# Routing and experts in one block, narrow expert blocks alternating with wide ones, and a head's first query job behind its second score group

## The reference

```python
xn = _layernorm(x, axis=-1)
# attention: 8 query heads of width 128 over one shared key/value head, causal, with a position table
q = (xn @ Wq + bq) + pe;  k, v = split(xn @ Wkv + bkv);  k = k + pe
probs = softmax(where(causal, (q @ k.T) / sqrt(128), -inf));  s = concat_heads(probs @ v) @ Wo
# mixture of 8 experts, the best 2 per token
logits = xn @ router_w + router_b;  gating = softmax(only the top 2 logits)
h = relu(xn @ w1[e] + b1[e]);  y = h @ w2[e] + b2[e]      # 256 -> 1024 -> 256
g = silu(sum over the two experts of gating * y)
out = x + s * g
```

## Time and profile before

| | |
|---|---|
| median of 3 runs (lowest, highest) | 1114.44 us (1110.93, 1115.57) |
| the profiled execution, its span | 1122.9 us, 1121.1 us |
| routing | 0 to 88.8 us |
| experts | 88.8 to 483.1 us |
| attention, with its tail from 1084 on | 483.1 to 1121.1 us |
| TensorE busy, share of the span | 1016.8 us, 91% |
| VectorE busy | 883.5 us, 79% |
| ScalarE, GpSimd busy | 554.5 us, 442.7 us |

### The profile page before, as it was taken

The page is one execution under the profiler, slowest core; times in us unless marked ns, Lnnn a source line. Parts: engine busy times, 40 slices in busy tenths (PEclk is TensorE's granted clock), DMA queues, the critical chain, the costliest instruction groups (busy, mean ns, idle before and its releaser), DMA issues.

```text
span 1121.1 us, 28441 instructions
## 1 busy us (share of the span) xinstructions
PE 1016.8 (91%) x10270; PEld 811.9 (72%) x10270; DVE 883.5 (79%) x1607; ACT 554.5 (49%) x1264; POOL 442.7 (39%) x499
## 2 busy tenths in 40 slices
PE   2536999999999999998989889999999999999997
PEld 1525888888888898755666667667777777777776
DVE  6894676676676454479999999998999999999972
ACT  3812223323323333346766666656666666666740
POOL 0013999899995100012323233333333333333331
PEclk9999999999999999998999999999999999999999
DMA  8547666756665512129987898988999888999993
GB/s 280 184 174 152 171 170 172 185 162 178 180 166 145 95 44 49 30 71 161 170 139 145 135 172 159 159 148 156 161 172 179 144 151 149 166 161 159 171 160 105
DMA packets 405896, 169.02 MB, mean 151 GB/s; under 512 B 348634, under 2 KB 396324, under 8 KB 405124
## 3 DMA queue, kind: packets, MB, share of 16 engines
q1 hardware_dynamic: 348704, 127.05, 57.0%
q10 hardware_dynamic: 50580, 22.45, 8.8%
q0 software_dynamic: 6480, 17.70, 7.4%
HBM read 51.66 MB, written 30.67 MB: 73 GB/s over the span
## 4 chain that ended last, share of the span: by engine, by line
DVE 27%; PE 20%; ACT 4%; issue 3%; DMA 2%; SPq 1%; ACTq 0%; DVEq 0%
DVE b_ph L1353 10%; DVE b_nmax L1314 8%; PE b_psO L1137 7%; PE b_psS L1118 5%; DVE b_outs L1361 2%; PE b_psJ L1075 2%; PE b_psJ L1151 2%; DVE b_psJ L1323 2%; ACT b_pr L1217 2%; PE b_psS L1162 2%; DMA b_pT<-b_ph 2%; ACT b_ph L1249 1%; PE b_psS L1075 1%; DVE b_Q L1337 1%; DVE b_f L1367 1%
## 5 line engine op out<-in xcount | busy, mean ns | idle before, releaser
L1442 POOL TENSOR_SCALAR b_ph<-b_pr,b_rrec 128x896 f16<-128x896 f32 (+4 forms) x160 | 109.3, 691 | 502.3 <-DVE b_rrec L1343 460.6
L938 ACT ACTIVATE h<-psU,bias 128x256 f32<-128x256 f32 (+1 forms) x320 | 125.1, 448 | 294.5 <-PE psU L858 170.4
L1217 ACT ACTIVATE b_pr<-b_psS,b_nmax 128x1024 f32<-128x1024 f32 (+7 forms) x256 | 187.3, 736 | 159.0 <-DVE b_nmax L1314 159.0
L1137 PE MATMUL b_psO<-b_pT,b_vp 128*128 128x128 f16 x3456 | 219.1, 221 | 20.5 <-DMA b_pT<-b_ph 20.4
L1137 PEld LDWEIGHTS b_psO<-b_pT,b_vp 128*128 128x128 f16 x3456 | 202.5, 99 | 29.6 <-issue 19.0
L858 PE MATMUL psU<-bxT,w_p 128*128 128x256 f16 (+1 forms) x1536 | 208.3, 273 | 16.5 <-DVE w_p L261 12.8
L1118 PE MATMUL b_psS<-b_kp,b_Q 128*128 128x512 f16 (+3 forms) x1152 | 220.2, 328 | 0.1
L1353 DVE SCALAR_TENSOR_TENSOR b_ph<-b_pr,b_rrec,b_ph 128x1024 f16<-128x1024 f32 (+7 forms) x256 | 209.9, 851 | 0.0
L871 PE MATMUL psY<-w_p,hp 128*128 x1512 | 206.4, 273 | 0.0
L959 DVE CAST hp<-h 128x512 f16<-128x512 f32 (+1 forms) x160 | 85.9, 537 | 137.1 <-ACT h L938 135.0
L1314 DVE TENSOR_REDUCE b_nmax<-b_psS 128x1 f32<-128x1024 f32 (+7 forms) x256 | 183.3, 748 | 8.6 <-PE b_psS L1121 8.6
(11 more groups left out here) (184 smaller groups left out, 1138.8 us busy)
## 6 DMA issues: line engine op xcount, KB each, us to landing
wstage<-in_L_ffn_w SPq DMA_DIRECT2D x48, 256.0 KB
expert_rows<-rowx SPq DMA_DIRECT2D x67, 128.0 KB
expert_outputs<-y ACTq DMA_DIRECT2D x31, 256.0 KB, 3.3
a_x_all<-in_L_attn_x SPq DMA_DIRECT2D x8, 512.0 KB, 9.8
a_w_raw<-in_L_ffn_w SPq DMA_DIRECT2D x4, 1024.0 KB, 6.4
xn_split<-a_xp SPq DMA_DIRECT2D x4, 1024.0 KB, 5.0
b_pT<-b_ph SPq DMA_TRANSPOSE x256, 3.7
xn_turned<-a_xT SPq DMA_DIRECT2D x3, 1024.0 KB, 13.0
```

The source lines that it names most:

```text
L938: a = eng.activation(h32[w % 4][:, g, 0:rows], psU[w % U][:, g, 0:rows], ACT.Relu, bias=bias[:, ds(e * HT + 2 * q + g, 1)], scale=1.0 / WS)
L1137: mm = eng.matmul(psO[w % 2][:, (u % 2) * P:(u % 2 + 1) * P], vb[:, a, j, :], pT[u][:, c * (u + 1) + j, :], start=(j == 0 and kk == 0), st ...
L1217: a = eng.activation(pr[k % 3][:, o:o + w], psS[BUF[i]][:, :, :].rearrange("p a n -> p (a n)")[:, o:o + w], ACT.Exp, bias=nmax[:, at:at + ...
L1442: a = eng.tensor_scalar(ph[k % 4][:, 2 * o:2 * o + w], pr[k % 3][:, o:o + w], rrec[:, at:at + 1], 1.0, ALU.mult, ALU.mult)
```

## The change

1. **One block.** `prologue` becomes `routing` and shares one block with `experts`: each engine runs its routing stream and goes on into its experts stream without meeting the others. A semaphore `own_` takes over what the meeting guaranteed for `blk_e`: PE, ACT and DVE wait for it. `owners` moves behind `who` on DVE. The PSUM banks of the routing are those of the experts.
2. **Narrow among wide.** A list `ORDER` gives the order of the blocks: 22 wide ones, then nine pairs of a wide and a narrow one. Gathers, stores and loads follow it (`FLOW`, `places_of`). On PE the narrow block's `up` alternates, matmul by matmul, with the wide block's `down`, and the next wide block's `up` with the narrow block's `down`.
3. **First query job later.** From head 1 on the first query job is issued at i = 1 in place of i = 0, behind `scores(n, 1)` and ahead of `values(n-1, 0)`; the key or value job of i = 1 follows it, ahead of `values(n-1, 0)` too. The second query job stays at i = 2, behind `values(n-1, 1)`. ACT and DVE treat the first job one step later, that of the keys or values in the same step as before.
4. **Tail.** `o_tile(TILES - 1)` moves behind `rows_out(3, 0, HEADS - 1)`.

The diff without its changed indentation, cut to its core:

```diff
+    own_ = whole.enter_context(nc.semaphore("owners_known"))
...
-        eng.indirect_dma_start(rowx[n % 4][:, :], None, xp_d, bass.IndirectOffsetOnAxis(ap=who[:, n:n + 1], axis=0)).then_inc(gx_[n % 4], 16)
+        eng.indirect_dma_start(rowx[n % 4][:, :], None, xp_d, bass.IndirectOffsetOnAxis(ap=who[:, FLOW[n]:FLOW[n] + 1], axis=0)).then_inc(gx_[n % 4], 16)
...
+    PLAIN = TWIN - (NBLK - TWIN)
+    ORDER = list(range(PLAIN)) + [b for j in range(NBLK - TWIN) for b in (PLAIN + j, TWIN + j)]
     def units_of(n):
-        return (2 * n, 2 * n + 1) if n < TWIN else (n + TWIN,)
+        b = ORDER[n]
+        return (2 * b, 2 * b + 1) if b < TWIN else (b + TWIN,)
+    FLOW = [m for n in range(NBLK) for m in units_of(n)]
...
-        prologue(nc, locals())
-        experts(nc, locals())
+        front(nc, locals())
...
             for s in range(CHUNKS):
                 one_hots(s)
-            owners()
             eng.wait_ge(s_sp, 1)
             eng.tensor_scalar(who[:, :], psJ[:, 0:UNITS], float(T * 2), None, ALU.add).then_inc(v["who_"], 1)
+            owners()
...
+            ahead = n - 1
+            twin = n and len(units_of(ahead)) == 2
+            even = n < NBLK and twin and len(units_of(n)) == 2
                 for g in range(HT):
-                    if TWIN < n < NBLK:
-                        narrow(n, g)
-                    elif n < NBLK:
-                        up(n, g)
-                    if n and n <= TWIN:
-                        down(n - 1, g)
-                    elif n == NBLK and g % 2:
-                        down(n - 1, g // 2)
-                    known = min(NBLK, n + 2 + max(0, n + 11 - TWIN))
+                    rooms(n, g)
+                    if n == 0 or even:
+                        for k in range(3 * DC):
+                            up(n, g, k)
+                    if n and twin and g < PAIR:
+                        halves_in(ahead, g)
+                    if n and not twin and g % 2 == 0:
+                        halves_in(ahead, g // 2)
+                    for k in range(3 * DC):
+                        if 0 < n < NBLK and not even:
+                            up(n, g, k)
+                        if twin:
+                            down(ahead, g // PAIR, 2 * (g % PAIR) + k // 3, k % 3)
+                        elif n and k % 2:
+                            down(ahead, 0, g, k // 2)
+                    known = min(NBLK, n + 2 + max(0, n - 8))
...
-            if n == 0:
-                job, bank = (("V", 0, 0), ("V", 0, 1), ("Q", 2, 0), ("Q", 2, 1), None)[i], ("J", "O0", "O1", "J", "")[i]
-            elif i in (0, 2) and n + 2 < heads:
-                job = ("Q", n + 2, i // 2)
-            elif i == 1 and n % HEADS >= 4 and HEADS * (b + 1) < heads:
-                job, bank = ("KKVV"[n % HEADS - 4], b + 1, n % 2), "S"
+            if n == 0 and i < 4:
+                self.add(k, (("V", 0, 0), ("V", 0, 1), ("Q", 2, 0), ("Q", 2, 1))[i], ("J", "O0", "O1", "J")[i])
+            elif n and i in (1, 2) and n + 2 < heads:
+                self.add(k, ("Q", n + 2, i - 1), "J")
+            if i == 1 and n % HEADS >= 4 and HEADS * (b + 1) < heads:
+                self.add(k, ("KKVV"[n % HEADS - 4], b + 1, n % 2), "S")
...
+            def work(q, k):
+                n, bank = k // 5, jobs.bank[q]
+                if jobs.freed(q):
+                    eng.wait_ge(jl_, jobs.freed(q))
+                if bank == "S":
+                    eng.wait_ge(ex_, 5 * n)
+                if n == 0:
+                    eng.wait_ge(pl_, {"J": 4, "O0": 5, "O1": 6}[bank])
+                if k % 5 == 1 and bank == "J" and n >= HEADS + 2:
+                    eng.wait_ge(ot_, n - HEADS - 1)
+                project(*jobs.order[q], job_bank[bank]).then_inc(jm_, 1)
...
                     scores(n, i)
+                    if n and i == 1:
+                        for q in jobs.at.get(k, ()):
+                            work(q, k)
                     if n and i:
                         values(n - 1, i - 1)
+                    if n == 0 or i != 1:
+                        for q in jobs.at.get(k, ()):
+                            work(q, k)
...
-            o_tile(TILES - 1)
             eng.wait_ge(ex_, LAST - 1)
             eng.wait_ge(al_, 4 * (NH - 1))
             rows_out(3, 0, HEADS - 1)
+            o_tile(TILES - 1)
```

More of the change, by code:

```diff
@@ new lines, in routing @@
+    L, L2, slot = (sb(s, [P, NT, E], F32) for s in ("L", "L2", "slot"))
+    both, oh = (sb(s, [P, 2, NT, E], F32) for s in ("both", "oh"))
+    cand, oh0, oh1 = both[:, 0], oh[:, 0], oh[:, 1]
+    tri16 = sb("tri16", [P, PARTS, TRI], F16)
+    tot16 = sb("tot16", [P, PARTS * P], F16)
+    over = Arena(v["nc"], v["table_at"])
+    lane16 = over.take("a_lane16", [P, P, PER], F16)
+    unit16 = over.take("a_unit16", [P, UNITS, PER], F16)
+    assert over.at <= v["w_at"]
+    ids16 = sb("ids16", [P, NT], F16)
@@ new lines, in routing @@
+    at_ = sb("at", [P, 2, NT], F32)
+    ix = [at_[:, i] for i in range(2)]
+    ex = sb("ex", [P, 3, NT], F32)
+    se = [sb(f"scane{i}", [P, 2, E], F32) for i in range(2)]
+    nbl = sb("nbl", [P, 2, E], F32)
+    q_i = sb("q_i", [P, 2, NT], U32)
+    cmpb = sb("cmpb", [P, max(NBLK, 2 * MOST) * E], F32)
+    bf = sb("bf", [P, 2, NBLK], F32)
+    ends, lim, move, last = (sb(s, [P, E], F32) for s in ("ends", "lim", "move", "last"))
+    first = sb("first", [P, 1], F32)
+    assert area.at <= v["top_at"]
@@ new lines, in routing, with before, turned @@
+    (s_b, s_bz, s_rh, s_rl, s_lg, s_ch, s_pos, s_diff, s_pick, s_tot, s_t16, s_cnt, s_e, s_oh, s_sp) = map(sem, (
+        "bias_turned", "bias_kept", "rw_hi", "rw_lo", "logits", "chain", "slots_known",
+        "top_diff", "picked", "totals", "totals_kept", "counted", "exp_diff", "one_hot", "slots_placed"))
+    def before(p, some):
+        return sum(1 for i in range(p + 1) if i in some)
+    def turned(p):
+        return xTb_next[:, 2 * p:2 * p + 2] if p < QT // 2 else xT[:, 2 * p - QT:2 * p - QT + 2]
@@ new lines, in on_gpsimd, with front, sem, _ @@
+    def on_gpsimd(eng):
+        for n in range(4, AHEAD + 4):
+            v["gather"](eng, n)
+        p = FIRST
+        eng.wait_ge(wd_, FIRST)
+        eng.wait_ge(v["xk_"], 48)
+        for n in range(AHEAD + 4, UNITS):
+            v["gather"](eng, n)
+            if p < v["ALL"]:
+                v["split"](eng, p)
+                p += 1
+    return on_tensor, on_scalar, on_vector, on_gpsimd, on_sync
+def front(nc, v):
+    with ExitStack() as ctx:
+        def sem(name):
+            return ctx.enter_context(nc.semaphore(name))
+        psU = [ctx.enter_context(nc.psum_tensor(f"psU{i}", [P, 2, 2 * P], F32)) for i in range(6)]
+        psY = [ctx.enter_context(nc.psum_tensor(f"psY{i}", [P, 2, 2 * P], F32)) for i in range(2)]
+        route, expert = routing(v, ctx, sem, psU), experts(v, ctx, sem, psU, psY)
+        block = ctx.enter_context(nc.Block())
+        @block.tensor
+        def _(eng):
+            route[0](eng)
+            expert[0](eng)
+        @block.scalar
+        def _(eng):
+            route[1](eng)
+            expert[1](eng)
+        @block.vector
+        def _(eng):
+            route[2](eng)
+            expert[2](eng)
+        @block.gpsimd
+        def _(eng):
+            route[3](eng)
+            expert[3](eng)
@@ L985, in _ @@
-        @block.gpsimd
-        def _(eng):
-            for n in range(4, AHEAD + 4):
-                v["gather"](eng, n)
-            p = FIRST
-            eng.wait_ge(wd_, FIRST)
-            eng.wait_ge(v["xk_"], 48)
-            for n in range(AHEAD + 4, UNITS):
-                v["gather"](eng, n)
-                if p < v["ALL"]:
-                    v["split"](eng, p)
-                    p += 1
+            route[4](eng)
+            expert[4](eng)
 def attention(nc, v):
```

1068 lines of the change are left out of this document (499 added, 569 removed).

## The result

The changed kernel takes 1127.95 us (median of 4 runs, 1124.28 to 1132.02) beside 1114.2 for the kernel before in the same runs: ratio 1.0113, 95% interval 1.0079 to 1.0147. It is slower by 1.1%; the forecast was 1126 us, in a range from 1112 to 1136. The profiled execution has a span of 1130.2 us; the one of before had 1121.1.

The account below looks back on a forecast made before the run. In the attention PE and DVE were both taken as close to their limit, with PE's matmul rate counting in the experts. Span 1121.1 + 25 - 9.5 - 4 = 1132.6 us, +11.5 on the median 1114.4: 1126 us, range 1112 to 1136.

Parts of the forecast that it names:

- The largest term: Attention heads 10 to 29: PE waits 1.7 us for DVE ahead of each second query job, 25.7 us in all.
- (a): Attention: the second query job's wait doesn't bind, DVE's low half being done in time; 1092 us, faster; chance 0.11.
- (b): Attention: hidden PE slack lets only about 0.6 us a head reach the end; 1113 us, no change; chance 0.10.
- Rival (d): Attention: PE's clock falls in the new waits in half of 20 heads, +15 to +30; 1145 us; chance 0.06.
- Heads 0 to 9: Early attention heads: up to +4 us from late scores, up to -5 from covered transpose waits; taken as -1.
- Part 2: Experts, narrow blocks among wide: a pair of steps takes 15.8 us at full speed; gain 9.5 us.
- rival (c): Experts: the instruction stream limits the mixed steps too, part 2 giving 0 to 3 us; 1134 us; chance 0.12.
- Part 1: Start of the experts, routing joined in one block: PE starts at about 86.2 in place of 90.18; taken as -4.
- block 2's wait stays: Experts: PE's wait of 3.6 us for block 2's rows stays about as long; if gone, 5 us more gained.
- The sum: Whole kernel: span 1132.6 us, +11.5, applied to the median 1114.4 gives 1126 us.
- the tail: End of the attention, output tile behind the last rows (part 4): between -2 and +1 us, taken as 0.

Follow-up runs that it names:

- low_first: Changed kernel with DVE doing the first query job's low half ahead of the maxima, ACT its high half ahead of the weighting: 1099.61 us, ratio 0.9865.
- front_alone: Changed kernel with the query jobs, attention and tail of the kernel before: 1103.5 us, ratio 0.9885.
- one_block_alone: Changed kernel with the jobs, tail and block order (wide first, narrow last) of the kernel before: 1110.95 us, ratio 0.9962.
- front_short_lead: Changed kernel with the jobs and tail of before, and POOL's gathers 9 units ahead of the weight splits, not 12: 1107.19 us, ratio 0.9892.
- const_weights: Kernel before with every expert matmul taking its weights from a constant address, those of expert 0: 1104.73 us, ratio 0.9902.
- jobs_alone: Kernel before with only the query jobs and tail of the changed kernel: 1140.29 us, ratio 1.022.

## Why the prediction was right, and where it was not

**The largest term: right in mechanism, 1.54 to 1.7 in size.** The forecast put the second query job 2.25 us behind the start of the values; the row of after shows 2.20, and of each link in it what was summed: 0.20, 1.20, 0.74 and 0.06. The wait reads 1.54 and not 1.7, as the profile counts from the modelled end of the values, 0.16 us after the next matmul could start. The same 0.16 explains the head: I took PE's own work as 18.04 - 0.34 = 17.70, but that gap too counts from a modelled end. With 17.70 - 0.16 = 17.54 the sum is 17.54 + 1.69 = 19.23, and 19.25 was measured. Forecast: 19.4 and 20.7; measured: 19.25 and 20.54 to 20.59. Over 20 heads the mis-sized term is 25.7 against 21.1 us. Some 2.9 of these 4.6 us are the 0.16; the rest is that the 20 heads took 374.4 us in the execution of before, and not the 372.7 that 12 heads of 18.04 and 8 of 19.52 to 19.57 make (one of them took 20.64).

**Rivals (a) and (b)**, that the wait doesn't bind or binds by half, are out: `low_first` comes near what (a) would have been (heads of 17.95 us where (a) had 17.70), and it needed the swap on DVE that (a) named as its condition.

**Rival (d), the clock.** It didn't fall behind the waits of 1.54 us in heads 10 to 29 (the windows of 700 to 900 and 900 to 1100 show 1.00 and 0.99). It did behind longer ones in the early heads: 0.56 over 521 to 524, behind two waits of 1.11 and 0.96 us with six values between them, 0.81 over 540 to 543, behind one of 2.18. Rows 12 had it between 1.42 and 3.44. The trace of before holds cases between these that the forecast left out: a granted clock of 0.58 over 564.51 to 567.51 behind a wait of 1.99 us and 0.71 over 659.36 to 662.36 behind one of 2.38, but 1.00 over 1084.37 to 1087.37 behind one of 2.06. So the rival lay nearer than "3.44 against 1.42" makes it look.

**Heads 0 to 9: right in number by luck.** I took -1 and the two profiles show -1.1. But in four other kernels with the attention of before this stretch took 176.8 (`front_alone`), 175.2 (`one_block_alone`), 176.9 (`front_short_lead`) and 179.4 us (`const_weights`), against 182.2 in the execution that I had read; with the new jobs it took 181.1 and 180.8 (`jobs_alone`). With the joined front the new jobs so stand some 4 to 6 us above the old ones, with the old front between 1.4 below and 1.4 above. The forecast's steps for this stretch, up to +4 from late scores and up to -5 from covered waits, are neither shown nor refuted, because one execution differs from the next by as much.

**Part 2**: -7.9 against -9.5. The pair took 16.2 us, not 15.8. Four of the eight pairs took 15.8 to 16.0, three 16.1 to 16.2, and one 17.9, with a wait of 1.05 us for ACT that I did not follow further. The other steps with 96 matmuls took 7.9 to 8.3 us. I read that as the stream being at its limit in them, as rival (c) said of the whole order, and refilling in the steps with 72; no run with constant addresses in the mixed order tests it. Rival (c) had 0 to 3 us; 8 were gained.

**Part 1**: the start at 86.06 against 86.2 forecast. That block 2's wait stays was wrong in the changed kernel, where it was absent, and right in `one_block_alone` (1.27 us); what I had not seen is that an earlier PE meets POOL's splits at 275 us, 0.5 to 3.7 us of waiting. The runs of `one_block_alone` (-1.8 to -6.7) fit the forecast's -4 and don't test it closely.

**The sum**: 1126 against 1127.95, inside 1112 to 1136. Between the two profiles the large term was 4.6 us too high, the tail 2.5 too low, and experts and start together right to 0.1: +9.1 in place of +11.5. The medians differ by 13.7, and the 4.6 us between the two are in no stage that I can name. So the mechanism was right and its size nearly so, but that the sum met the median within 2 us is partly luck.

## What to carry to other kernels

Where two producers write the same PSUM bank, look at what the releasing engine has queued between them: a wait is paid not for the distance on the producer's engine, but for every operation ahead of the release on the other one. Moving the release ahead of one 1.2 us operation was worth 2.5% here; moving the producer away only handed the wait to the bank's next user. And before a stage is read from one execution, look at that stage in other kernels that leave it alone: the execution of before had 3 to 7 us of its own in the early heads.

## What the runs showed of the hardware

- In the narrow steps, matmuls with weight addresses from registers came at 93.5 ns each, with two register operations of 46 ns for every three matmuls on PE's queue; with constant addresses, and all else the same, they came at 74.5 ns, the pace at which the first of these steps had started (74.9). The limit shows in steps of 128 columns and not in wide ones (109 ns a matmul).
- PE's clock after a wait: it kept 2.4 GHz (granted 0.99 to 1.00) behind 20 waits of 1.54 us. Behind longer ones both happened. It fell towards 1.2 GHz (means of 0.51 to 0.71 over the 3 us behind) after 1.99, 2.38 and 2.75 us in the kernel before, 1.99 and 2.18 in the kernel after and 2.49 in `low_first`, and kept 1.00 behind 2.06 in the kernel before, 2.29 and 2.36 in `jobs_alone`, 2.46 in `one_block_alone` and 2.74 in `low_first`. `jobs_alone` has a fall to 0.61 behind waits of 0.48 and 1.60 us with six matmuls of values between them. The length of a wait alone doesn't decide.
- A modelled matmul end lies 0.16 us behind the point where the next can start (six of 512 columns: 1.46 us long, the next starts 1.30 us after their start, 665.42 to 666.72 in the kernel before). Gaps read in the timeline are short by that much.
